# Feed-forward down products: whole fp32 factors in four 32-column strips in place of three products of fp32r halves

## The reference, cut to what matters

```python
for i in range(L):                       # L = 2
    ...                                  # retention gives Y, [B, S, 256]
    Yn = _layernorm(Y, ln2_w[i], ln2_b[i])
    X = jax.nn.silu(Yn @ ffn_w1[i] + ffn_b1[i]) @ ffn_w2[i] + ffn_b2[i] + Y
```

## Time and profile before

| | before |
|---|---|
| median of 3 runs | 1413.55 us (1413.16 to 1413.99) |
| profiled execution: its own time | 1412.88 us |
| profiled execution: span of the trace | 1411.1 us |
| mean granted clock of TensorE | 0.997 of full speed |
| busy share: PE, PEld, DVE, ACT, POOL | 97%, 82%, 76%, 65%, 57% |

### The profile page before, as it was taken

One profiled execution on the slowest core, in us unless ns is written; L12 is line 12 of the kernel. 1 busy time (PEld: TensorE's weight loads), 2 busy tenths in 40 slices (PEclk: granted clock), 3 DMA queues, 4 the chain that ended last, 5 costly groups with the idle time before them and its releaser, 6 DMA issues. The chain is left out here.

```text
span 1411.1 us, 38230 instructions
## 1 busy us (share of the span) xinstructions
PE 1362.4 (97%) x13900; PEld 1159.9 (82%) x13900; DVE 1073.2 (76%) x2349; ACT 920.4 (65%) x1874; POOL 802.5 (57%) x882
## 2 busy tenths in 40 slices
PE   6999999999998999999999999999999999989998
PEld 5788887898997888888899988887777878768886
DVE  6888897664547888895755669776999999978775
ACT  4666665565553556555655557786788888778775
POOL 3767766412104676663743437776666666637774
PEclk9999999999999999999999999999999999999999
DMA  6100000100001000000410010000000000000001
GB/s 218 50 3 1 0 2 2 38 1 0 1 1 61 2 3 0 1 2 2 126 40 16 0 43 1 1 0 2 2 2 0 0 0 0 1 1 16 31 30 46
DMA packets 21182, 26.36 MB, mean 19 GB/s; under 512 B 1985, under 2 KB 19137, under 8 KB 20929
## 3 DMA queue, kind: packets, MB, share of 16 engines
q1 hardware_dynamic: 20768, 24.61, 5.4%
q10 hardware_dynamic: 288, 0.07, 0.0%
HBM read 20.48 MB, written 4.19 MB: 17 GB/s over the span
## 5 line engine op out<-in xcount | busy, mean ns | idle before, releaser
L560 DVE TENSOR_TENSOR ffn_h_lo<-ffn_h,ffn_h_hi 128x512 fp32r<-128x512 f32 x112 | 87.6, 782 | 120.3 <-ACT ffn_h_hi L779 120.3
L778 ACT ACTIVATE ffn_h<-ffn_hp,c_b 128x512 f32<-128x512 f32 x112 | 77.2, 689 | 145.3 <-PE ffn_hp L881 144.8
L560 DVE TENSOR_TENSOR ternary_ffn_h_lo<-ternary_ffn_h,ternary_ffn_h_hi 128x512 fp32r<-128x512 f32 x128 | 105.6, 828 | 64.6 <-ACT ternary_ffn_h_hi L779 64.4
L1294 POOL TENSOR_TENSOR ret_qk<-ret_qk,ret_qk_sin 128x512 f32<-128x512 f32 x64 | 93.5, 1461 | 96.7 <-DVE ret_qk_sin L1401 96.7
L2292 POOL TENSOR_TENSOR win_rms<-win_sq_sum,win_minus_half 128x20 f32<-128x20 f32 x30 | 106.3, 3542 | 62.1 <-DVE win_sq_sum L2411 59.0
L894 PE MATMUL ternary_ffn_yp<-down_ternary,ternary_ffn_h_hi 128*128 128x256 f32 x512 | 130.7, 288 | 1.0 <-DVE ternary_ffn_h_lo L560 1.0
L894 PE MATMUL ternary_ffn_yp<-down_ternary,ternary_ffn_h_lo 128*128 128x256 f32 x512 | 127.5, 282 | 0.0
L894 PE MATMUL ffn_yp<-down_hi,ffn_h_hi 128*128 128x256 f32 x448 | 127.5, 284 | 0.0
L894 PE MATMUL ffn_yp<-down_hi,ffn_h_lo 128*128 128x256 f32 x448 | 125.0, 279 | 0.0
L894 PE MATMUL ffn_yp<-down_lo,ffn_h_hi 128*128 128x256 f32 x448 | 124.9, 279 | 0.0
L456 POOL TENSOR_TENSOR ternary_ffn_h_sq<-ternary_ffn_h_sq 128x512 f32<-128x512 f32 x61 | 92.2, 1519 | 30.9 <-ACT ternary_ffn_h_sq L788 27.1
(11 more groups left out here) (336 smaller groups left out, 4655.7 us busy)
## 6 DMA issues: line engine op xcount, KB each, us to landing
staging<-in_w SPq DMA_DIRECT2D x4, 1024.0 KB, 6.4
ffn_x_in<-in_x SPq DMA_DIRECT2D x8, 512.0 KB, 3.7
X<-in_x SPq DMA_DIRECT2D x7, 512.0 KB, 8.1
out<-X SPq DMA_DIRECT2D x7, 512.0 KB, 2.9
staging<-in_wqkv SPq DMA_DIRECT2D x2, 768.0 KB, 4.7
rotary<-in_rotary SPq DMA_DIRECT2D x1, 1024.0 KB, 7.2
staging<-in_w_up SPq DMA_DIRECT2D x1, 1024.0 KB, 5.2
staging<-in_w_down SPq DMA_DIRECT2D x1, 1024.0 KB, 7.7
```

The source lines that it names most:

```text
L560: nc.vector.tensor_tensor(h_lo[:, m % R, :], h[:, m % R, :], h_hi[:, m % R, :].bitcast(F32), ALU.subtract).then_inc(h_ready, 1)
L778: nc.scalar.activation(h[:, m % R, :], hp[m % 2][:, :], fn, bias=bias)
L1294: nc.gpsimd.tensor_tensor(whole_, whole_, qk_sin[:, r, :, :, :], ALU.add).then_inc(qk_done, 1)
```

## The change

The down products of the dense feed-forward stages (in `ffn` with begun=True and in the drain of `retention`) take h and the weights as plain fp32. `by_strips` issues, for each tile t of 128 rows, four matmuls with whole fp32 operands: strip i has the 32 rows 32i to 32i+31 of the tile as its stationary columns and writes partitions 32i to 32i+31 of the output; all four stream the same 256 columns of the weights. ScalarE evaluates the Silu once, `hidden_low` and the halves of ffn_w2 are gone, the product waits for h_read of ScalarE, and ffn_w2 is loaded straight into `down` in place of `staging`. The ternary stages keep their two products of halves.

```diff
+STRIP = 32
...
+def by_strips(nc, out, x, w, start, stop):
+
+    for at in range(0, P, STRIP):
+        strip = slice(at, at + STRIP)
+        last = nc.tensor.matmul(out[strip, :], x[:, strip], w, start=start, stop=stop)
+    return last
...
-                        if to_do(b):
+                        if ternary and to_do(b):
                             hidden_low(b, m)
...
-                at_least(act, h_ready, MF * b + m - R + 1)
+                if ternary:
+                    at_least(act, h_ready, MF * b + m - R + 1)
...
-                nc.scalar.activation(h[:, m % R, :], hp[m % 2][:, :], fn, bias=bias)
+                whole = nc.scalar.activation(h[:, m % R, :], hp[m % 2][:, :], fn, bias=bias)
+                if not ternary:
+                    whole.then_inc(h_read, 1)
+                    return
                 nc.scalar.activation(h_hi[:, m % R, :], hp[m % 2][:, :], fn, bias=bias).then_inc(h_read, 1)
...
-            down_passes = [(h_hi, w) for w in down] + [(h_lo, down[0])]
+            down_passes = [(h_hi, down), (h_lo, down)] if ternary else [(h, down)]
...
             def down_product(b, m, k, between=None):
-                pe.wait_ge(h_ready, MF * b + m + 1)
+                pe.wait_ge(h_ready if ternary else h_read, MF * b + m + 1)
...
-                        last = nc.tensor.matmul(yp[k][t // 2][:, (t % 2) * D:(t % 2 + 1) * D],
-                                                x[:, m % R, t * P:(t + 1) * P], w[:, m, :],
-                                                start=(m == 0 and t % 2 == 0 and n == 0),
-                                                stop=(m == MF - 1 and t % 2 == 1 and last_pass))
+                        product = nc.tensor.matmul if ternary else partial(by_strips, nc)
+                        last = product(yp[k][t // 2][:, (t % 2) * D:(t % 2 + 1) * D],
+                                       x[:, m % R, t * P:(t + 1) * P], w[:, m, :],
+                                       start=(m == 0 and t % 2 == 0 and n == 0),
+                                       stop=(m == MF - 1 and t % 2 == 1 and last_pass))
...
-        h, h_hi, h_lo = scratch
+        h = scratch
...
-        HALVES = {(1, 5): 0, (1, 6): 1, (1, 7): 2, (N, 1): 3, (N, 2): 4, (N, 3): 5, (N, 5): 6, (N, 6): 7}
+        HALVES = {(1, 5): 0, (1, 6): 1, (1, 7): 2, (N, 1): 3}
...
-                nc.scalar.activation(h[:, m % R, :], hp[m % 2][:, :], ACT.Silu, bias=bias)
-                nc.scalar.activation(h_hi[:, m % R, :], hp[m % 2][:, :], ACT.Silu, bias=bias).then_inc(h_read, 1)
+                nc.scalar.activation(h[:, m % R, :], hp[m % 2][:, :], ACT.Silu, bias=bias).then_inc(h_read, 1)
...
             def down_product(m):
-                pe.wait_ge(h_ready, m + 1)
-                passes = [(h_hi, next_down[0]), (h_hi, next_down[1]), (h_lo, next_down[0])]
+                pe.wait_ge(h_read, m + 1)
+                if m == 0:
+                    pe.wait_ge(prefetched, 16 * len(loads))
                 for t in range(TB):
-                    for at, (x, w) in enumerate(passes):
-                        last = nc.tensor.matmul(next_y[t // 2][:, (t % 2) * D:(t % 2 + 1) * D],
-                                                x[:, m % R, t * P:(t + 1) * P], w[:, m, :],
-                                                start=(m == 0 and t % 2 == 0 and at == 0),
-                                                stop=(m == MF - 1 and t % 2 == 1 and at == len(passes) - 1))
+                    last = by_strips(nc, next_y[t // 2][:, (t % 2) * D:(t % 2 + 1) * D],
+                                     h[:, m % R, t * P:(t + 1) * P], next_down[:, m, :],
+                                     start=(m == 0 and t % 2 == 0), stop=(m == MF - 1 and t % 2 == 1))
...
-            down = pair("down", [P, MF, D], c)
+            down = sb("down", [P, MF, D], at=c)
```

More of the change, by code:

```diff
@@ L12 @@
 from contextlib import ExitStack
+from functools import partial
 import numpy as np
@@ L142, in ffn @@
         h = sb("h", [P, R, BT])
-        h_hi = sb("h_hi", [P, R, BT], F32R)
-        h_lo = sb("h_lo", [P, R, BT], F32R)
         if ternary:
+            h_hi = sb("h_hi", [P, R, BT], F32R)
+            h_lo = sb("h_lo", [P, R, BT], F32R)
             table_set = sb("table_set", [P, 1])
@@ L759, in _ @@
             if begun:
-                dve.sem_inc(h_ready, MF)
                 dve.sem_inc(y_done, YD)
@@ L1120, in retention @@
         next_xt_read, h_full, h_read = sem("next_xt_read"), sem("h_full"), sem("h_read")
-        h_ready, h_used, next_y_full = sem("h_ready"), sem("h_used"), sem("next_y_full")
+        h_used, next_y_full = sem("h_used"), sem("next_y_full")
         prefetched = sem("prefetched")
@@ L1485, in next_input_low @@
                 nc.vector.tensor_tensor(xt_lo[:, 1, j, :], xt[:, j, :], xt_hi[:, 1, j, :].bitcast(F32), ALU.subtract)
[L1487 to L1491, removed]
             def next_residual():
@@ L1504, in drain @@
                 gated_low(NH - 3)
-                hidden_low(0)
                 next_normalise()
                 residual(NH - 3, i, NH - 3 - 4 * i)
-                hidden_low(1)
                 square_sums(NH - 1)
-                hidden_low(2)
                 gated_low(NH - 2)
-                hidden_low(3)
                 residual(NH - 2, i, NH - 2 - 4 * i)
                 gated_low(NH - 1)
-                hidden_low(4)
-                hidden_low(5)
                 residual(NH - 1, i, NH - 1 - 4 * i)
@@ L1519, in drain @@
                 next_input_low(1)
-                hidden_low(6)
-                hidden_low(7)
                 next_residual()
@@ L2902, in hybrid_block @@
         ret_stages = [staged([d[n][layer] for n in ("wqkv", "wg", "wo")]) for layer in range(L)]
-        ffn_stages = [staged([d[n][layer] for n in ("w1", "w2")]) for layer in range(L)]
+        ffn_stages = [staged([d["w1"][layer]]) for layer in range(L)]
         ternary_stages = staged([d["w_up"], d["w_down"]])
@@ L2935, in hybrid_block @@
                           for st in ret_stages]
-            ffn_halves = [[pieces(st[0], up, (every, j, slice(a * BT, (a + 1) * BT))) for j in range(KD) for a in range(2)] +
-                          [pieces(st[1], down, (every, slice(2 * m, 2 * m + 2), every)) for m in range(MF // 2)]
+            ffn_halves = [[pieces(st[0], up, (every, j, slice(a * BT, (a + 1) * BT))) for j in range(KD) for a in range(2)]
                           for st in ffn_stages]
@@ L2944, in hybrid_block @@
                             for st, t in zip(ternary_stages, (up_t, down_t))]
-            for_hidden = (staging[:, 0:4 * BT].rearrange("p (r n) -> p r n", n=BT),
-                          up_t[:, :, :].rearrange("p k (r n) -> p (k r) n", n=BT),
-                          down_t[:, :, :].rearrange("p (r m) n -> p r (m n)", r=4))
+            for_hidden = staging[:, KD * FF:KD * FF + 4 * BT].rearrange("p (r n) -> p r n", n=BT)
             used = ()
@@ L2953, in hybrid_block @@
                 used = retention(nc, f"ret{layer}", X, ident, lane, qkv=qkv, gate=gate, out_w=out_w,
-                          norm=kept["ln1"][:, layer], gn=kept["gn"][:, layer], loads=ffn_stages[layer],
+                          norm=kept["ln1"][:, layer], gn=kept["gn"][:, layer],
+                          loads=ffn_stages[layer] + [(whole(down), d["w2"][layer].rearrange("(m p) n -> p m n", p=P))],
                           halves=ffn_halves[layer], next_norm=kept["ln2"][:, layer],
@@ L2977, in hybrid_block @@
                           sq_sum=sb("win_sq_sum", [P, NH]), rms=sb("win_rms", [P, 3, NH]), rot=sb("win_rot", [P, 2, NH, WD]))
-        used = ffn(nc, "ternary_ffn0", X, ident, lane, retired=used, up=(up_t,), down=(down_t,), loads=list(win_stage.values()),
+        used = ffn(nc, "ternary_ffn0", X, ident, lane, retired=used, up=(up_t,), down=down_t, loads=list(win_stage.values()),
             halves=[(win_stage["win_wqkv"][0][:, j, :], win_qkv[0][:, j, :], win_qkv[1][:, j, :]) for j in range(KD)],
@@ L2986, in hybrid_block @@
                          win_rotary=win_stage["win_rotary"][0], **for_window)
-        ffn(nc, "ternary_ffn1", X, ident, lane, retired=used, up=(up_t,), down=(down_t,), out_dram=out_blocks)
+        ffn(nc, "ternary_ffn1", X, ident, lane, retired=used, up=(up_t,), down=down_t, out_dram=out_blocks)
 def lay_out(i):
```

1 line of the change is left out of this document (removed).

## The result

| | before | changed |
|---|---|---|
| median | 1413.55 us | 1492.51 us (1492.49 to 1495.99, 3 runs) |
| ratio to before | | 1.056, 95% interval 1.054 to 1.059 |
| profiled execution: its own time | 1412.88 us | 1495.99 us |
| profiled execution: span | 1411.1 us | 1494.2 us |
| mean granted clock | 0.997 | 0.994 |

The kernel became 79.0 us slower; 81.2 were forecast (1494.7, in a range of 1476 to 1510).

A forecast was written before the change was run, and what follows sets the result against it. The prediction took TensorE's issue of matmuls to bound the feed-forward stages. Products +42.2, going into and out of strips +41.5 and starts behind transposes -2.5 sum to +81.2 us, a median of 1494.7 us, range 1476 to 1510.

The forecast's parts named there:

- the case that I took: Whole kernel: TensorE pays for the products and for switching, +81.2 us, 1494.7 us; given 87%.
- Term 1: Down products: whole fp32 streams its columns four times, 1.73 us a piece in place of 1.40, 128 pieces, +42.2 us.
- Term 2: Feed-forward stages and drains: going into strips and out again, 0.34 us for each of 122 runs, +41.5 us.
- Term 3: Runs behind fp32 transposes: a start the down product already pays goes, 28 x 0.09, -2.5 us.
- The bound: Feed-forward stages: time is TensorE's issue of matmuls; its changes count in full, VectorE's and ScalarE's savings are hidden.
- What was costed at nothing: VectorE's dropped subtractions, ScalarE's second Silus, the ffn_w2 halves, earlier h and the ffn_w2 load: 0 us.
- Other stages move by more than 2 us: Sign of a wrong prediction: stages other than dense feed-forward and drains should stay equal.
- Hidden switching: Rival: operands ready early and early weight loads hide switching in strip runs; only +42.2 us stays, 1456 us; 6%.
- loads that don't overlap: Rival: each record set of a down product waits for its own weights, 113 us more, 1608 us; 4%.
- The price by record: Rival: strips are paid by record, not column; a piece costs 0.88 us in place of 1.40, 1386 us; 2%.
- That nothing would change: Rival: the change doesn't do what it says, down products stay as they are; no change; 1%.
- The range: Whole kernel: 1476 us without the first-product delay and 5 us of waits; above, slower strips, +17 us, 1512; taken as 1476 to 1510.

The follow-up runs named there:

- pairs: Changed kernel with the dense feed-forward stages' down products issued two by two, behind every second up product: 1476.31 us, ratio 1.044.
- relief_kept: Changed kernel with the second Silu and the subtraction still done in the dense feed-forward stages, results unused, TensorE waiting for the subtraction: 1492.60 us, ratio 1.055.
- whole_array: Changed kernel with each down product as one whole fp32 product over all 128 columns in place of four strips: 1453.98 us, ratio 1.028.
- split_runs: Changed kernel with each down product cut in two, tiles 0 and 1 in the middle of the up product: 1528.19 us, ratio 1.081.

## Why the prediction was right

The forecast was 1494.7 us and the median 1492.51, so 2.2 us were forecast too much, and the case that I took is the one that came. That it came so near is in part luck: terms 1 and 2 were 4.7 us too large, and term 3, which should have been nothing, took 2.5 of them off again.

- **The bound.** That TensorE's issue alone counts in these stages held: the stages grew by what TensorE got, and the run with the relief kept away shows no difference.
- **Term 1**, +42.2 us for four passes of the columns. The kernel with products over all columns has this term alone and is 39.8 us slower than before. The price of a set, 0.432 us, was right (records follow each other by 0.216). Three small things make up the 2.4 us. A step without transposes grew from 2.807 to 3.128 us (medians of the records in the two traces), 0.32 us where rounded times had given 0.33, which is 1 us in 128 pieces. The first feed-forward stage had a wait of 0.7 us for transposes, which is gone. And the retention stages became 0.4 us shorter each ahead of their drains; no run here shows why.
- **Term 2**, +41.5 us for 122 runs of 0.34 us. The count was two too high, 0.7 us, and the price about right. The timeline has 0.33 going in where 0.23 is usual, and 0.34 between the first two products after; the runs with half and with twice as many give 0.32 to 0.33 a run. Two rows of one place each had been enough for it. Between the kernel with products over all columns and the changed one lie 38.5 us, 0.32 for each of 120.
- **Term 3**, -2.5 us behind transposes, was wrong in kind, though small. I had read 0.21 us between the first two down products in place of 0.12 as a price. In the run pairs four transposes and the up product behind them can be followed:

```profile
305.60 0.60 PE L924 MATMUL ffn_tp<-c_ident,xn 128*128 128x128 f32 x4
305.95 0.48 PE L894 MATMUL ffn_hp<-xt_hi,up_hi 128*128 128x512 f32 x1
306.26 0.40 PE L894 MATMUL ffn_hp<-xt_hi,up_lo 128*128 128x512 f32 x1
```

  From 305.60 to 306.26 are 0.66 us, and four transposes of 0.109 with one product of 0.233 make 0.67. The product starts early and its follower is late by as much; nothing was there to be saved. Where strips come behind transposes they cost their going in like anywhere else:

```profile
305.89 0.60 PE L924 MATMUL ffn_tp<-c_ident,xn 128*128 128x128 f32 x4
306.42 1.93 PE L77 MATMUL ffn_yp<-down,ffn_h 128*32 128x256 f32 x32
```

  In the changed kernel that is 0.53 us for four transposes, 0.44 of them their own. So the term should have been 0.
- **What was costed at nothing.** The lighter engines gave nothing in the feed-forward stages (relief_kept). No run tests the load of ffn_w2 into `down` alone; in the changed kernel's list of waits TensorE waits for no transfer. "Other stages move by more than 2 us" was to be a sign of a wrong prediction, and the last one moved by 3.1 us in the profiled execution: that is the low clock, since without it in whole_array the stage is within 0.8 us of the time before. Ternary 0 has 147.7 us in both traces.
- **The rivals.** Hidden switching (1456 us) fell by split_runs and pairs; loads that don't overlap (1608 us) fell with sets 0.43 us apart. By that rule of the Trainium skill (TensorE: Matmul & The Clock Gate, Part 3: weight loads overlap only where row groups differ) each set would wait for its loads; the trace of the changed kernel, with 0.216 us from record to record, doesn't agree. The price by record (1386 us) fell with the 382 ns of 3584 records. That nothing would change fell with the 79.0 us.
- **The range.** Its upper end was set at 1510 us, while the sum ahead of it gives 1512; the measured time is far from both.

## What to carry to other kernels

A whole fp32 product costs four passes of its columns, over the whole array or in strips beside each other, and three products of fp32r halves cost 3.2 of such passes (0.350 against 0.431 us here); so strips give nothing to a factor that fills the array anyway. Each run of strips between products over the whole array costs a third of a microsecond here, going in and out together, so use strips in long runs, with neighbours in the queue on different columns, or not at all next to products over all columns. Where one engine is busy all the time and gets still more work, work taken off the others can be worth nothing (147 us of it here): look at the stretch, not at the sum of busy times.

## What was not expected of the hardware

- A product behind fp32 work over all columns (transposes or whole fp32 products) starts early and delays its follower by the same 0.1 to 0.2 us. Such a pair of rows must be read together with what stands ahead of it.
- TensorE overlapped strips that were not neighbours in the queue: with four products for the same 32 columns in a row, the next strip's products began when two of them were through. 16 products took 20 slots of 0.216 us and not 26.
- Grouping down products in the kernel before cost 5.5 us, of which 3.4 are waits of transposes for their input.
- The lower clock (0.50) appeared for 3.4 to 6.8 us at other places in each profiled execution: in the changed kernel near 38 us, in the attention and at the start of the last stage (in the kernel before in the attention alone, as long as TensorE had work). The changed kernel's execution with these was 3.5 us longer than its other two.
